# Graph layer with attention and residual norm: VectorE turns z2, GpSimd's queue loads the rounded adjacency

## What is computed

```python
type_sum = adj @ x                                   # both gates and x_b use the same sum
attn_a = sigmoid(concat([type_sum, x], 1) @ Wa.T + ba)
attn_b = sigmoid(concat([type_sum, x], 1) @ Wb.T + bb)
h = x @ W_sa
scores = (h @ a_sa[0, :512])[:, None] + (h @ a_sa[0, 512:])[None, :]
e = where(adj != 0, exp(-leaky_relu(scores, 0.01)), 0)
x_a = (e / (e.sum(1, keepdims=True) + 1e-5)) @ h
x_b = adj @ (x @ W_gcnb) + b_gcnb
g = sigmoid(attn_a * x_a + attn_b * x_b)
out = layernorm(x + g)
```

## Time and profile before

| | us |
|---|---|
| median of 3 runs | 962.42 (961.98 to 964.37) |
| profiled execution, its own time | 962.28 |
| span of that execution, first to last instruction | 960.4 |

### The profile page before, as it was taken

How to read it: one execution, slowest core, us unless ns; L and a number is a source line. 1 busy time by engine, 2 the same in 40 slices (tenths; PEclk the granted TensorE clock), 3 DMA queues, 4 the chain that set the end, 5 groups by cost and what they waited for, 6 DMA issues and landing times. The chain is left out here.

```text
span 960.4 us, 13001 instructions
## 1 busy us (share of the span) xinstructions
PE 943.9 (98%) x4368; PEld 783.6 (82%) x4368; DVE 672.0 (70%) x1264; ACT 440.7 (46%) x798; POOL 114.3 (12%) x328
## 2 busy tenths in 40 slices
PE   9999999999999999999999999999999999999996
PEld 6888887788788888888888888888888888888875
DVE  5979878875767676676676676685675675565667
ACT  5656644442544443543453453443543443454432
POOL 0000000220120120120120120120120120111112
PEclk9999999999999999999999999999999999999999
DMA  8677532333333433433434433333433333333320
GB/s 264 185 201 227 170 105 77 109 98 99 112 105 94 124 91 107 120 96 102 121 95 105 119 100 99 110 105 93 121 105 94 109 111 87 88 105 88 94 72 33
DMA packets 139555, 109.00 MB, mean 113 GB/s; under 512 B 10337, under 2 KB 113633, under 8 KB 139489
## 3 DMA queue, kind: packets, MB, share of 16 engines
q1 hardware_dynamic: 138624, 106.74, 39.2%
q10 hardware_dynamic: 864, 1.44, 0.7%
HBM read 101.32 MB, written 6.83 MB: 113 GB/s over the span
## 5 line engine op out<-in xcount | busy, mean ns | idle before, releaser
L595 PE MATMUL bank<-e_hi,x_hi 128*128 128x512 f32 (+1 forms) x728 | 273.3, 375 | 1.4 <-DVE e_lo L774 1.1
L597 PE MATMUL bank<-e_lo,x_hi 128*128 128x512 f32 (+1 forms) x728 | 272.4, 374 | 0.0
L596 PE MATMUL bank<-e_hi,x_lo 128*128 128x512 f32 (+1 forms) x728 | 272.2, 374 | 0.0
L399 ACT ACTIVATE e_hi<-u,c_col 128x512 fp32r<-128x512 f32 (+1 forms) x182 | 126.0, 692 | 258.0 <-DVE u L762 115.2
L620 PE MATMUL bank<-x_hi,adj_r 128*128 128x512 f32 x572 | 225.0, 393 | 0.0
L621 PE MATMUL bank<-x_lo,adj_r 128*128 128x512 f32 x572 | 223.0, 390 | 0.0
L774 DVE SCALAR_TENSOR_TENSOR e_lo<-u,c_col,e_hi 128x512 fp32r<-128x512 f32 (+1 forms) x182 | 130.0, 714 | 46.5 <-ACT e_hi L399 37.5
L595 PEld LDWEIGHTS bank<-e_hi,x_hi 128*128 128x128 f32 x728 | 137.0, 188 | 27.6 <-DVE e_lo L774 2.1
L406 ACT CAST adj_r<-raw 128x512 fp32r<-128x512 f32 (+1 forms) x180 | 105.1, 586 | 115.3 <-PE bank L621 98.8
L596 PEld LDWEIGHTS bank<-e_hi,x_lo 128*128 128x128 f32 x728 | 137.0, 188 | 24.9
L597 PEld LDWEIGHTS bank<-e_lo,x_hi 128*128 128x128 f32 x728 | 137.0, 188 | 24.6
(11 more groups left out here) (119 smaller groups left out, 848.3 us busy)
## 6 DMA issues: line engine op xcount, KB each, us to landing
raw<-adj_t_dram SPq DMA_DIRECT2D x158, 256.0 KB, 2.9
adj<-adj_t_dram SPq DMA_DIRECT2D x156, 256.0 KB, 2.9
out_dram<-y SPq DMA_DIRECT2D x24, 256.0 KB, 3.3
z1s<-x_dram SPq DMA_DIRECT2D x14, 256.0 KB, 5.2
adj<-adj_t_dram SPq DMA_DIRECT2D x26, 128.0 KB, 2.2
raw<-adj_t_dram SPq DMA_DIRECT2D x22, 128.0 KB, 2.4
z2s<-x_dram SPq DMA_DIRECT2D x6, 256.0 KB, 4.6
y<-x_dram SPq DMA_DIRECT2D x6, 256.0 KB, 3.8
```

The lines of the kernel that those rows point to most:

```text
L399: nc.scalar.activation(e_hi[g % E_RING][:, 0:cols(b)], u[g % U_RING][:, 0:cols(b)], ACT.Copy, scale=c_col[:, j:j + 1]).then_inc(e_hi_ready, 1)
L595: nc.tensor.matmul(z1[k][:, 0:n], x_hi[:, j, kk], e_hi[s][:, 0:n], start=(j == 0), stop=False)
L596: nc.tensor.matmul(z1[k][:, 0:n], x_lo[:, j, kk], e_hi[s][:, 0:n], start=False, stop=False)
L597: ins = nc.tensor.matmul(z1[k][:, 0:n], x_hi[:, j, kk], e_lo[s][:, 0:n], start=False, stop=(j == TILES - 1))
```

## The change

PE's `turn` stays for the last two tiles alone. For tiles 0 to 23, DVE transposes z2 at places 0 to 3 of tile t: at each place four 32x32-block transposes of 32 partitions x (4 x 32) columns, each into another group of 32 partitions of a new SBUF tile `z2t`. ACT and DVE split `z2t` rather than the PSUM bank. PE no longer waits at place 0 for the split of the tile before (`zt_lo_ready`); DVE has that wait, in its own order behind `z2_lo`.

The buffers `raw`, SP's `load_raw` and ACT's `adjacency` go. GpSimd's queue loads the adjacency straight into `adj_r` (three buffers, type float32r, rounded by the DMA); load m waits until PE has used chunk m - 3. GpSimd's queue now holds the loads in the order of `places()`, and `moments(t - 1)` stands at place 5 of tile t, behind that place's loads.

```diff
-RAW_RING = 2
-ADJ_R_RING = 2
+ADJ_R_RING = 3
+        z2t = sb("z2t", [P, KT, P])
...
-            def load_raw(m):
...
-            def adjacency(m):
...
-            for t in range(LAST - 1):
-                moments(t)
+            def load_adj_r(m):
+                if m > LAST_CHUNK:
+                    return
+                since(pool, adj_r_used, m - ADJ_R_RING + 1)
...
+                nc.gpsimd.dma_start(adj_r[m % ADJ_R_RING][:, 0:parts(m), :], source) \
+                    .then_inc(adj_r_loaded[m % ADJ_R_RING], 16)
+
+            for m in range(TILES + ADJ_R_RING):
+                load_adj_r(m)
+            for b, q, t, i, j, chunks in places():
+                for c in chunks:
+                    load_adj_r(chunk_number(t + 2, c) + ADJ_R_RING)
+                if i == 5 and t >= 1:
+                    moments(t - 1)
+            moments(LAST - 2)
...
-                nc.scalar.copy(zt_hi[:, :, :].rearrange("p k i -> p (k i)"), turned[:, :]).then_inc(zt_hi_ready, 1)
+                nc.scalar.copy(zt_hi[:, :, :], z2t[:, :, :]).then_inc(zt_hi_ready, 1)
...
-                pe.wait_ge(adj_r_ready, m + 1)
+                pe.wait_ge(adj_r_loaded[s], 16 * (m // ADJ_R_RING + 1))
...
-                if i == 0:
-                    since(pe, zt_lo_ready, 2 * t)
-                    turn(t, turned)
-                    if q == 0 and b > 1:
-                        pe.wait_ge(denoms, b)
+                if i == 0 and q == 0 and b > 1:
+                    pe.wait_ge(denoms, b)
...
+            def turn(t, a):
+                if a == 0:
+                    dve.wait_ge(z2_copied, t + 1)
+                    since(dve, zt_lo_ready, 2 * t)
+                rows = slice(32 * a, 32 * a + 32)
+                blocks = z2s[rows, t % 2, :].rearrange("p (k m i) -> p k m i", k=KT, m=4)
+                for m in range(4):
+                    ins = nc.vector.transpose(z2t[32 * m:32 * m + 32, :, rows], blocks[:, :, m, :])
+                if a == 3:
+                    ins.then_inc(turn_done, 1)
...
                     if q == 0:
                         denominators(b - 1)
+                if i < 4:
+                    turn(t, i)
                 if i == 1:
```

More of the change, by code:

```diff
@@ L116, in adj_resnorm_kernel @@
         adj = [sb(f"adj{s}", [P, WIDE, P]) for s in range(ADJ_RING)]
-        raw = [sb(f"raw{s}", [P, CHUNK, P]) for s in range(RAW_RING)]
         adj_r = [sb(f"adj_r{s}", [P, CHUNK, P], F32R) for s in range(ADJ_R_RING)]
+        z2t = sb("z2t", [P, KT, P])
         l_row = sb("l_row", [P, WIDE * P])
@@ L166, in adj_resnorm_kernel @@
         adj_loaded = [sem(f"adj_loaded{s}") for s in range(ADJ_RING)]
-        raw_loaded = [sem(f"raw_loaded{s}") for s in range(RAW_RING)]
+        adj_r_loaded = [sem(f"adj_r_loaded{s}") for s in range(ADJ_R_RING)]
         l_saved, l_loaded = sem("l_saved"), sem("l_loaded")
@@ L282, in _ @@
                 load_adj(j + ADJ_RING)
-                if FIRST_AFTER[j] is not None:
-                    load_raw(FIRST_AFTER[j] + 1)
                 if j == 7:
@@ L298, in _ @@
                     sp.dma_start(bias_row[:, :], b_gcnb.to_broadcast([P, D])).then_inc(bias_loaded, 16)
-            load_raw(TILES + 1)
             for b, q, t, i, j, chunks in places():
@@ L303, in _ @@
                     load_adj(b * TILES + j + ADJ_RING)
-                for c in chunks:
-                    load_raw(chunk_number(t + 2, c) + RAW_RING)
                 if i == 2 and t >= 2:
@@ L313, in _ @@
                         .then_inc(l_saved, 16)
-            for c in range(LAST_FIRST, CHUNKS):
-                load_raw(chunk_number(LAST, c) + RAW_RING)
             store(LAST - 3)
@@ L359, in moments @@
                     ins.then_inc(moment_steps if n < len(steps) - 1 else norm_ready, 1)
-            for t in range(LAST - 1):
-                moments(t)
+            def load_adj_r(m):
+                if m > LAST_CHUNK:
+                    return
+                since(pool, adj_r_used, m - ADJ_R_RING + 1)
+                if m < TILES:
+                    source = adj_t[0:WIDE, :, m, :].rearrange("t p i -> p t i")
+                else:
+                    t, c = chunk_of(m)
+                    j, n = chunk(c)
+                    source = adj_t[t, :, j:j + n, :]
+                nc.gpsimd.dma_start(adj_r[m % ADJ_R_RING][:, 0:parts(m), :], source) \
[8 more added lines that the diff above has]
+            moments(LAST - 2)
             for n in range(2):
@@ L497, in _ @@
                 pieces_hi(j)
-                if FIRST_AFTER[j] is not None:
-                    adjacency(FIRST_AFTER[j])
                 if j == TILES - 2:
@@ L516, in _ @@
                         steep(g + 1)
-                for c in chunks:
-                    adjacency(chunk_number(t + 2, c))
                 if i == 0 and t >= 1:
@@ L544, in _ @@
             gate_exps(LAST - 1)
-            for c in range(LAST_FIRST, CHUNKS):
-                adjacency(chunk_number(LAST, c))
             act.wait_ge(turn_done, LAST)
```

18 lines of the change are left out of this document (3 added, 15 removed).

## The result

The changed kernel takes 967.66 us (median; 963.12 to 970.55) beside 962.16 us for the kernel before on the same chips: 1.0045 times as long, interval 1.0030 to 1.0059. It is a little slower; 958.7 was forecast, and 967 was the end of the range. Its profiled execution took 965.99 us with a span of 964.2, 3.7 us more than before's 962.28.

The account below looks back on a forecast made before the run. PE was taken to bound the kernel, except tiles 0 and 1, where DVE sets the pace. -11.8 + 6.2 + 1.0 + 1.0 = -3.6 us on 962.28 gave 958.7 us, range 952 to 967.

Parts of the forecast that it names:

- PE's turns and the wait at tile 2: Tiles 1 to 23: 0.44 us saved per turn, 10.1 us, plus 1.66 us of tile 2's wait; together -11.8 us.
- tiles 0 and 1, with the copy of z1: DVE sets the pace there; two turns of transposes, less DVE's idle time, push PE: +6.2 us (3.6 to 10.6).
- block ends: DVE's later mask frees SP later, nearly cancelled by other effects: +0.5 us at each of two, +1.0 us (-1.5 to +2).
- start: Load 3 at the kernel's start waits until PE has used chunk 0 and lands late: +1.0 us (0 to +2).
- I count no loss of it: PE's clock, granted in full through the present stalls, was to stay so in tiles 0 and 1: no loss.
- the two block ends where l was last: The only block ends charged for a late row of l, +0.5 us each.
- d: DVE's time for one transpose of 32 partitions x 128 elements, without overlap: 0.28 us, 16 a tile.
- the two idles of 2.8 us: DVE's idle times of 1.19 and 1.63 us in tiles 0 and 1, taken to absorb part of two turns' transposes.
- counting nothing at tile 0: No gain from tile 0's turn: PE goes on only when ACT has copied z1 out, which comes no earlier.
- the overlap: First rival: transposes overlap at 0.20 us each, tiles 0 and 1 cost 3.6 us, time 955 us; chance 0.20.
- the double pass: Second rival: each block goes through DVE twice, 0.42 us a transpose, time 964.1 us; chance 0.16.
- the third rival: GpSimd's loads land late and PE waits for adj_r, first behind tiles of six places: 968.7 us; chance 0.12.

Follow-up runs that it names:

- e8c: The changed kernel with matmuls of no use on PE ahead of three weighted steps of tiles 0 and 1 and the column sums of blocks 1 to 4: 964.72 us.
- e6: The changed kernel with tiles 0 and 1 turned on PE and the l row saved three places earlier by SyncE: 947.43 us, 0.9855 of the kernel before.
- e10: The kernel before with GpSimd's loads and the l row saved three places earlier, all turns on PE: 959.12 us, 0.9968 of the kernel before.
- e4: The changed kernel with SyncE saving the next block's l row three places earlier: 957.80 us, 0.9961 of the kernel before.
- e8b: The changed kernel with matmuls of no use on PE ahead of three weighted steps of tiles 0 and 1: 968.64 us, 1.0063 of the kernel before.

## Why the prediction was wrong

Set against the spans (960.4 and 964.2), term by term. The 24 turns that lie in the stretches, at 0.49 each, and tile 2's 1.66 us stand in the first row, and are added back to the stretches of the others. The profiled execution lies 1.7 us below the median of 967.66; what the slower executions lost beside it no trace shows.

| term | predicted | measured | of it slow matmuls |
|---|---|---|---|
| PE's turns and the wait at tile 2 | -11.8 | -13.4 | |
| tiles 0 and 1, with the copy of z1 | +6.2 (3.6 to 10.6) | +10.7 | 1.7 |
| block ends | +1.0 (-1.5 to +2) | +6.9 | 2.8 |
| start | +1.0 (0 to +2) | 0.0 | |
| last tiles | none | -0.4 | |
| sum | -3.6 | +3.8 | 4.5 |

**The step that failed first is the sentence "I count no loss of it" on PE's clock.** I had argued from the full clock behind the waits of before. But those were at most 1.9 us before the last tiles (2.14 there, at full clock too), and the new ones in tiles 0 and 1 were 2.1 to 2.7; slow matmuls stood behind three of the changed kernel's waits there and behind two at block ends, one of them of only 1.10 us, so length alone does not decide. They cost 1.7 us in tiles 0 and 1 (after against e8c) and 14 x 0.2 = 2.8 us at the block ends, 4.5 of the 7.4 us by which the sum missed. This term had no bound in the range.

**The block ends were mis-sized.** The mechanism was named: SyncE freed by a mask that comes later, a row that lands late, e_hi, the running sum. At block 1 it came out near the forecast without the clock: the row left 8.3 us later than before, of which 7.1 is the kernel's own lateness by then, and the wait of PE was 2.18 us in place of 1.90. What I missed is what the later row does at the other ends, since I counted only "the two block ends where l was last": at blocks 2 and 3, where PE had not waited, it now waits 1.10 and 0.77 us, and at block 4 1.96 in place of 0.66. Before, ACT waited for the row in three of the five; now in all. Without the slow matmuls it is 4.1 us, twice the upper bound.

**Tiles 0 and 1 were right in kind and too small.** The term that was mis-sized is d. A quarter turn of four transposes puts DVE's next instruction 1.37 us later, 0.34 each and not 0.28. Eight of them less the two idles of 2.8 us are the 8.2 us by which the e_lo of tile 1's place 4 comes late. The rest of the 9.0 us that remain without the clock, some 1.0, are turns 0 and 1 in the first row of the table: PE waits for DVE in these tiles, so the time of its own turns was not won there, though the sum had booked tile 1's 0.44 us.

The late copy of z1 is no loss beside this. In ACT's queue the e_hi of step 27 stands ahead of the copies; it waits for DVE's mask, now behind the first quarter turn (131.00 to 132.23), and PE's first step of the block starts 1.17 us later, though a turn was taken from in front of it. But no wait of DVE follows from it, so it is part of the same 8.2 us, and counting nothing at tile 0 cost the sum nothing by itself.

**What held.** The matmuls of turns fell from 104 to 8, and a turn is worth 0.49 us (0.44 forecast). The price of a transpose lay at 0.31 to 0.34, so neither the overlap (0.20) nor the double pass (0.42) came true. By the Trainium skill's rule (page "VectorE: DVE Perf Modes", section "Two Vector instructions with no wait between them"), an instruction whose output starts in another quarter of the partitions than the last output is held until all before it have finished; four transposes in 1.25 us, at 303 ns each, agree. From tile 2 on the transposes are hidden: e6 gains 10.7 to 11.7 us over e10 with DVE at 83%. The loads land in 3.2 us (median; the slowest took 12.3), and no chunk waited for one behind the start, so the third rival fell: with the loads alone the kernel is 0.2% faster. The Trainium skill's rule that GpSimd is locked out while DVE runs in a two-port mode (page "SBUF — State Buffer", section "SBUF: two separate sides") did not show in these loads' landing; whether DVE ran such a mode here no row says. The start cost nothing, the lower bound. The wait before normalise was 1.2 us at most.

The prediction named as what would make it wrong "if PE stalls outside tiles 0 and 1 and the block ends". PE did not: the stalls lie at the places named (and, as before, in the last tiles), but there are more of them, they are longer, and a lower clock follows. Neither rival that ended slower had this mechanism.

## What to carry to other kernels

When work goes from the bounding engine to another, look first for the stretches in which the other is already the bound, and leave the work where it was there; two tiles of 24 and one early DMA made the difference between 0.45% slower and 1.4% faster. A wait on TensorE may cost more than its length: price a new wait of two or three us with the slow matmuls behind it (here 1.0 to 1.8 us a time where PE is the bound), and don't take a full clock behind shorter waits as proof. An operation that several engines reach in turn through queues (mask, load, row save, row load, e_hi, sum) shifts as a whole when its first link moves; count every place that it passes, also those with no wait yet.

## What the runs showed of the hardware

Over all traces of this study, slow matmuls followed all ten waits of PE of 3.0 to 3.2 us, four of six of 2.7, eight of 21 between 1.9 and 2.2, and two of the 38 between 1.0 and 1.8 (1.59 and 1.10 us). The same wait, at the same place, was followed by them in one kernel and not in another: 2.10 us at 132 in the changed kernel, with; the same 2.10 us in e4, without. They begin 0.3 to 2.3 us after PE has started again, and last 5 to 9 matmuls of 512 columns. What decides in the middle cases no run here tells. The time goes roughly with the clock from execution to execution: 963 to 970.5 us with clocks of 0.994 to 0.988 in the changed kernel, 947.3 to 948.4 in e6.

Why e8b, which took the slow matmuls from tiles 0 and 1, had a higher median than the changed kernel stays open. Its trace suggests that the block ends got the worse for it; with those filled too the time fell by 3.9 us, but the executions with the lowest clocks have no trace. The 0.4 us that the last tiles gave were not followed up.
